# Three seams of a four-stage kernel: a new order in the stencil's last batch, earlier weight and bias loads for attention, and thirty spare matrix products at the very end

## The chip, the cores and the metric

The program runs on one core of one Trainium2 chip. A time is the device time of one execution in microseconds (us); for the kernel before there are three of them and a fourth, profiled execution. Engines are named as the profile names them: PE is TensorE, DVE VectorE, ACT ScalarE, POOL GpSimd and SP SyncE, which here only issues DMAs. DMAs that SP issues all go through one queue (q1 in the profile).

## What is computed

Four layers, one after another, on x of shape (8, 512, 512), all in float32:

```python
# layer 0: a finite-difference step on each 512x512 grid, then max(.., 0)
gradv_Af  = _grad(Af[:, 0], 1) + _grad(Af[:, 1], 2)
gradvv_Bf = _grad2(Bf[:, 0], 1) + _grad2(Bf[:, 1], 2) + _grad(_grad(Bf[:, 2], 2), 1) + _grad(_grad(Bf[:, 2], 1), 2)
x = jnp.maximum(f + (-gradv_Af + gradvv_Bf * 0.5) * dt[:, None, None], 0.0)
# layer 1: attention with an adaptive layer norm (scale and shift from the timestep), bias, mask; then a feed-forward
x = _ln(src) * (1.0 + scale) + shift
q, k, v = x @ Wq + bq, x @ Wk + bk, x @ Wv + bv          # 16 heads of 32
probs = softmax(where(mask, -inf, q k^T / sqrt(32) + attention_bias))
x = x + ((probs v) @ Wo + bo)
x = x + _gelu2((_ln(x) * g2 + beta2) @ W1 + b1) @ W2 + b2
# layer 2: for each batch element one of eight experts: gelu feed-forward, residual, layer norm
# layer 3: hidden + strength * response; response = (hidden @ basis @ basis[:32]^T) @ resp_w^T + biases,
#          basis from two Gram-Schmidt orthogonalisations, strength from a gate on the mean over the rows
```

`_grad` and `_grad2` use one-sided formulas in the first and last row and column, and these make work of their own below.

## The kernel before, in words

The program has three blocks: `stencil` (layer 0), `attention` (the first half of layer 1) and `feed_forwards` (the rest of layer 1 with layers 2 and 3). Between two blocks stands a barrier of all engines. Inside a block each engine runs its own list of instructions, in the order written, and waits on semaphores. No scheduler reorders anything: the Python order of an engine's function is its order on the chip.

**stencil.** The loop goes over the 8 batch elements n. For each, DVE makes the products V, Qp, Qm, Xp, Xm (L508, L593, L595, L512, L513), PE sums them with small band matrices in `acc[n % 2]` (L410 to L425), DVE adds the sum of element n-1 to y (`final(n - 1)`, L532) and makes the centre product y of n (L617, semaphore `s_tf`), and ACT takes the maximum with zero (`relu`, L372, for the last element L368). Rows 0 and 511 of each grid need a one-sided formula. Their ingredients are written to DRAM (`edge(n)`, L244, six small DMAs; `border_pre(n)`, L251, two), collected for four elements at a time (`load_edges`, L270, `load_border_pre`, L276), put together on DVE in 14 tiny steps (`edge_step`, L545 to L553), and stored (`store_borders`, L283). The second of these two groups needs element 7 and so comes at the block's end. `relu(n)` waits until both DMAs of `border_pre(n)` have landed (`s_row`), since it overwrites y; `store(n)` (L257, the last one L261) waits for relu.

The end of this block also prepares attention: SP loads batch 0 of x back in token order into `shared[0]` (L305), the row of scale and shift (L309), Wq into `shared[2]` and Wk into `shared[1]` (L311). DVE takes mean and variance (`first_rows`, L559 to L566), POOL the power -1/2, ACT scales Wq by 1/sqrt(32) (L380) and normalises the rows (L383), and DVE applies scale and shift (L570, L573).

**attention.** Every weight is split into a high part (ACT, `weights_high`, L964) and the rest (DVE, `weights_low`, L1228), and a product is three PE instructions (`split_matmul`, L96 to L98). The opening makes q, k and v of batch 0 and the first scores; then a loop over batch elements and 64 units each runs. Wv and Wo are staged in float32 through `shared[2]` and `shared[1]` after Wq and Wk have left them. DVE scales the q bias by 1/sqrt(32) (L1326) once four POOL-issued DMAs have landed (`s_const`).

**feed_forwards.** 16 passes (8 elements in layer 1, 8 in layer 2) of 16 units; POOL makes high weights (`high`, L1648), DVE the rest (`low`, L1990). DVE normalises the first rows (`ln_apply`, L2017), PE transposes them (L1831). After the last pass come residual, statistics, layer norm (L2055 to L2173), 16 PE transposes (`last_y_transposes`, L1894), high and low parts yH, yL (L1774, L2181), projections to 32 features (L96 to L98), the gate (L1908), and the response rows (L1921, L2200), which SP stores.

Of the kernel before, what the change touches and what calls it, by code (L numbers as in the profile page):

```python
# [38 lines left out]
def f32(ap):  # L39

    return ap.bitcast(F32)
# [73 lines left out]
def stencil(nc, a, x_out, edges, ada_rows, shared, s_rows, s_weights, first):  # L115
# [11 lines left out]
    with ExitStack() as ctx:  # L127
# [57 lines left out]
        s_ndt = sem("dt_negated")  # L185
        s_coef = sem("coefs_made")
# [34 lines left out]
        def _(sp):  # L221
# [62 lines left out]

            for n in range(B):
# [16 lines left out]
            sp.wait_ge(s_sum, B - 1)  # L302
            sp.wait_ge(s_eout[0], 32)
            for r in range(R):
                sp.dma_start(shared[0][:, r, :], tokens_at(x_out, 0)[:, r, :]).then_inc(s_rows[r], 16)  # L305
            sp.wait_ge(s_ada, 16)
            sp.wait_ge(s_tf, B - 1)
            for k, tile in enumerate(first_scale_shift):
                sp.dma_start(tile, ada_rows[0:1, k].to_broadcast([P, D])).then_inc(first.s_ab, 16)  # L309
            for tile, name, loaded in zip(shared[2:0:-1], ("Wq", "Wk"), s_weights):  # L310
                sp.dma_start(tile[:, :, :], a[f"L1_cond_{name}"].rearrange("(k p) n -> p k n", p=P)).then_inc(loaded, 16)  # L311
# [9 lines left out]
        def _(pool):  # L321
# [18 lines left out]
            identity(pool, first.ident, first.s_id)  # L340
            pool.memset(first.mhalf[:, :], -0.5).then_inc(first.s_half, 1)
# [7 lines left out]
        def _(act):  # L349
# [79 lines left out]
        def _(dve):  # L429
# [126 lines left out]
            def first_rows():  # L556
# [9 lines left out]
                dve.tensor_scalar(first.var[:, :], first.mv[:, :, 1], 1e-5, None, ALU.add).then_inc(first.s_var, 1)  # L566
                dve.wait_ge(first.s_ab, 32)
# [14 lines left out]
            for n in range(B):  # L582
# [1733 lines left out]
```

## Time and profile before

| what | value |
|---|---|
| median of 3 executions | 2751.28 us (2749.57 to 2753.77) |
| profiled execution, its own time | 2753.89 us |
| its span in the trace | 2752.2 us |
| PE busy | 2642.5 us, 96% |
| DVE, ACT, POOL busy | 1695.0, 1024.9, 1027.7 us |
| stencil, to attention's first instruction | 0 to 221.4 us |
| attention | 221.4 to about 1187 us |
| feed_forwards, with the tail from 2723.1 | about 1187 to 2752.2 us |

The span counts from the first to the last instruction that the trace shows; the execution's own time is 1.7 us longer. Times below are places in that span. PEclk is the clock that TensorE was granted: 1.00 is 2.4 GHz, 0.50 is 1.2 GHz.

### The profile page before, as it was taken

Reading aid. Unit: us, or ns where it says so; the run is one execution under the profiler, and the core shown is the slowest. Engines: PE = TensorE matmul, PEld = TensorE weight load, DVE = VectorE, ACT = ScalarE, POOL = GpSimd, SP = SyncE. Lnnn points to the kernel's source line nnn. Section 1 sums busy time; section 2 is a strip of 40 time slices with the busy share of each in tenths; the row PEclk is TensorE's granted clock in tenths of the full one; section 3 lists DMA queues with packets and bytes.
Section 4 is the critical chain, followed back from the end, with each engine's and each line's share of the span. In section 5 each row is a group of like instructions: output and inputs, shape, how many; then the busy total and the mean of one; then the engine's idle time right before and its main releaser. Section 6 shows DMA issues by size and latency. Waiting matters only on the chain. (4 is left out here: it accounts for less than half of the span.)

```text
span 2752.2 us, 46368 instructions
## 1 busy us (share of the span) xinstructions
PE 2642.5 (96%) x17096; PEld 2036.1 (74%) x17096; DVE 1695.0 (62%) x3379; ACT 1024.9 (37%) x2161; POOL 1027.7 (37%) x771
## 2 busy tenths in 40 slices
PE   7986999999999999989999999999999999999997
PEld 2434777777777777667888888888787888888775
DVE  8975777777777777765444444445554564565443
ACT  1124666666666666611111111111222323323322
POOL 3003777776777777542101110022222322332210
PEclk9997999999999999999999999999999999999998
DMA  4334564655646456532011001104333243243311
GB/s 169 115 119 149 163 196 139 189 154 174 195 139 190 145 183 183 154 98 77 1 31 31 18 14 31 31 9 124 115 104 119 95 134 124 94 125 127 106 44 39
DMA packets 217922, 306.00 MB, mean 111 GB/s; under 512 B 20450, under 2 KB 98402, under 8 KB 215012
## 3 DMA queue, kind: packets, MB, share of 16 engines
q1 hardware_dynamic: 215954, 302.00, 35.2%
q8 instruction: 138, 2.26, 0.3%
q0 software_dynamic: 1744, 1.04, 0.2%
q14 instruction: 86, 0.70, 0.1%
HBM read 268.94 MB, written 34.04 MB: 110 GB/s over the span
## 5 line engine op out<-in xcount | busy, mean ns | idle before, releaser
L910 POOL TENSOR_TENSOR at_bias<-at_bias,at_mask 128x1024 f32<-128x1024 f32 x220 | 471.7, 2148 | 249.1 <-DMA at_bias<-in_fside_Bx16xSxS 247.7
L1286 DVE CUSTOM_DVE_ANT_0 at_bias<-at_bias,at_bank_score 128x512 f32<-128x512 f32 x512 | 337.8, 680 | 186.2 <-PE at_bank_score L1139 140.8
L96 PE MATMUL ff_bank_out<-ff_WH,ff_gH 128*128 128x512 f32 x1024 | 408.0, 398 | 1.9 <-DVE ff_gL L2037 1.9
L96 PE MATMUL ff_bank_hid<-ff_hH,ff_WH 128*128 128x512 f32 x1024 | 402.7, 393 | 2.7 <-DVE ff_WL L1990 2.6
L1763 ACT ACTIVATE ff_g<-ff_bank_hid,plain_b1c 128x512 f32<-128x512 f32 x256 | 175.6, 686 | 606.2 <-PE ff_bank_hid L98 606.2
L98 PE MATMUL ff_bank_out<-ff_WH,ff_gL 128*128 128x512 f32 x1024 | 400.1, 391 | 0.0
L97 PE MATMUL ff_bank_hid<-ff_hL,ff_WH 128*128 128x512 f32 x1024 | 400.1, 391 | 0.0
L98 PE MATMUL ff_bank_hid<-ff_hH,ff_WL 128*128 128x512 f32 x1024 | 399.6, 390 | 0.0
L97 PE MATMUL ff_bank_out<-ff_WL,ff_gH 128*128 128x512 f32 x1024 | 399.1, 390 | 0.0
L2037 DVE TENSOR_TENSOR ff_gL<-ff_g,ff_gH 128x512 fp32r<-128x512 f32 x256 | 179.0, 699 | 351.1 <-ACT ff_g L1763 346.7
L1648 POOL TENSOR_SCALAR ff_WH<-shared 128x1024 fp32r<-128x1024 f32 x144 | 181.4, 1260 | 564.8 <-PE ff_bank_out L98 346.2
L999 ACT ACTIVATE at_prob<-at_bias,at_nmax 128x512 f32<-128x512 f32 x512 | 366.5, 716 | 20.1 <-DVE at_nmax L1286 19.9
L1146 PE MATMUL at_bank_probT<-first_ident,at_prob 128*128 128x128 f32 x2048 | 313.5, 280 | 5.8 <-ACT at_prob L999 5.4
L1146 PEld LDWEIGHTS at_bank_probT<-first_ident,at_prob 128*128 128x128 f32 x2048 | 228.1, 141 | 94.0 <-issue 67.2
L2035 DVE CAST ff_gH<-ff_g 128x512 fp32r<-128x512 f32 x128 | 70.7, 553 | 359.9 <-ACT ff_g L1763 359.8
L1762 ACT ACTIVATE ff_gH<-ff_bank_hid,plain_b1c 128x512 fp32r<-128x512 f32 x128 | 88.3, 690 | 520.4 <-PE ff_bank_hid L98 520.3
L1007 ACT ACTIVATE at_probT<-at_bank_probT 128x512 f32<-128x512 f32 x256 | 153.2, 598 | 271.1 <-PE at_bank_probT L1146 159.7
L96 PEld LDWEIGHTS ff_bank_hid<-ff_hH,ff_WH 128*128 128x128 f32 x1024 | 193.0, 188 | 45.3 <-DVE ff_WL L1990 3.5
L98 PEld LDWEIGHTS ff_bank_hid<-ff_hH,ff_WL 128*128 128x128 f32 x1024 | 193.0, 188 | 41.1
L98 PEld LDWEIGHTS ff_bank_out<-ff_WH,ff_gL 128*128 128x128 f32 x1024 | 192.5, 188 | 41.6
L97 PEld LDWEIGHTS ff_bank_hid<-ff_hL,ff_WH 128*128 128x128 f32 x1024 | 193.2, 189 | 39.9
L96 PEld LDWEIGHTS ff_bank_out<-ff_WH,ff_gH 128*128 128x128 f32 x1024 | 192.8, 188 | 39.2 <-DVE ff_gL L2037 2.3
(316 smaller groups left out, 4296.0 us busy)
## 6 DMA issues: line engine op xcount, KB each, us to landing
at_bias<-in_fside_Bx16xSxS SPq DMA_DIRECT2D x256, 512.0 KB, 3.8
shared<-in_L_cond_Wi SPq DMA_DIRECT2D x128, 256.0 KB, 2.7
shared<-in_L_cond_Wo SPq DMA_DIRECT2D x128, 256.0 KB, 2.9
shared<-x_after_layer SPq DMA_DIRECT2D x64, 256.0 KB, 5.0
st_f<-in_x SPq DMA_DIRECT2D x8, 1024.0 KB, 7.0
x_after_attention<-shared SPq DMA_DIRECT2D x32, 256.0 KB, 2.6
shared<-in_L_cond_W SPq DMA_DIRECT2D x32, 256.0 KB, 2.9
shared<-x_after_attention SPq DMA_DIRECT2D x32, 256.0 KB, 4.4
```

Source lines behind the costliest of these rows:

```text
L96: pe.matmul(out, wh, xh, start=first, stop=False)
L97: pe.matmul(out, wh, xl, start=False, stop=False)
L98: return pe.matmul(out, wl, xh, start=False, stop=last)
L910: pool.tensor_tensor(bias[i % NB][:, :, :], bias[i % NB][:, :, :], mask[:, i // 2 % R, :].unsqueeze(1).to_broadcast([P, 2, S]), ALU.add).t ...
L999: act.activation(prob[u % 2][:, :], bias[u // 2 % NB][:, u % 2, :], ACT.Exp, scale=-1.0, bias=nmax[:, u % 4:u % 4 + 1], accum_out=sums[:, ...
L1007: act.activation(probT[g % 2][:, j].rearrange("p k q -> p (k q)"), pT[0][:, :], ACT.Copy).then_inc(s_pt[0], 1)
L1146: t = pe.transpose(pT[u % 2][:, k * P:(k + 1) * P], prob[u % 2][:, k * P:(k + 1) * P], ident[:, :])
L1286: dve.tensor_tensor_reduce(t, t, pS[u % HC][:, :], -1.0, 3.0e38, ALU.add, ALU.min, nmax[:, u % 4:u % 4 + 1]).then_inc(s_max, 1)
L1648: pool.tensor_scalar(WH[:, f, :], stage[f % 2][:, :], 1.0, 0.0, ALU.mult, ALU.add).then_inc(s_wh, 1)
L1762: act.activation(gH[f % 2][:, :], pg[f % 2][:, :], func, bias=column).then_inc(s_gh, 1)
L1763: act.activation(g32[f % 2][:, :], pg[f % 2][:, :], func, bias=column).then_inc(s_g32, 1)
L2037: dve.tensor_tensor(gL[f % 2][:, :], g32[f % 2][:, :], f32(gH[f % 2][:, :]), ALU.subtract).then_inc(s_g, 1)
```

## The change

Six edits, at the seams between the blocks.

1. In the stencil SP reloads batch 0 (`load_first_rows`) ahead of `edge(7)`, and loads scale, shift, Wq and Wk (`load_first_weights`) right behind `edge(7)`. Before, both stood behind `store(6)`.
2. DVE takes the first rows' statistics ahead of `final(6)`, applies scale and shift (`scale_first_rows`) behind the centre product of element 7, and runs all 14 edge steps after `final(7)`. Before: statistics, scale and shift, 12 edge steps, `final(7)`, 2 edge steps.
3. ACT normalises the rows ahead of `relu(6)` and scales Wq after it.
4. The q, k and v biases are loaded by POOL at the start of the stencil into a tile that outlives it, and the q bias is scaled in the stencil. Attention's opening waits for them no longer. Wv is loaded as attention's first DMA, into `probT[0]`, which is not yet in use; Wo goes to `shared[2]` as soon as Wq has left it.
5. In feed_forwards POOL starts `high(0)` only after the first rows are normalised, and makes its constants after `high(2)`.
6. Behind the last output product PE runs 30 spare products (`SPARE`) that nobody reads. The tail's high and low parts go to `hH` and `hL`, four buffers each and by then free, so that ACT and DVE wait for no projection.

```diff
+            def load_first_rows():
+                sp.wait_ge(s_sum, B - 1)
+                sp.wait_ge(s_eout[0], 32)
+                for r in range(R):
+                    sp.dma_start(shared[0][:, r, :], tokens_at(x_out, 0)[:, r, :]).then_inc(s_rows[r], 16)
...
             for n in range(B):
                 if n == EG:
                     load_edges(0)
+                if n == B - 1:
+                    load_first_rows()
                 edge(n)
+                if n == B - 1:
+                    load_first_weights()
...
-                if n == B - 1:
-                    act.wait_ge(s_weights[0], 16)
-                    act.activation(shared[2][:, :, :], shared[2][:, :, :], ACT.Copy, scale=1.0 / math.sqrt(HD)).then_inc(first.s_ws, 1)
+                if n == B - 2:
                     act.wait_ge(first.s_rstd, 2)
...
+                if n == B - 1:
+                    act.wait_ge(s_weights[0], 16)
+                    act.activation(shared[2][:, :, :], shared[2][:, :, :], ACT.Copy, scale=1.0 / math.sqrt(HD)).then_inc(first.s_ws, 1)
                 relu(n)
...
+                if n == B - 1:
+                    first_rows()
                 if n > 0:
                     final(n - 1)
...
-            first_rows()
-            for k in range(12):
-                edge_step(1, k)
+            scale_first_rows()
             final(B - 1)
-            for k in range(12, 14):
+            for k in range(14):
                 edge_step(1, k)
...
+            load_weight(2, "Wv")
             load_mask(0)
             for i in range(3):
                 load_bias(0, i)
-            for k, name in ((2, "Wv"), (3, "Wo")):
-                sp.wait_ge(s_wl, k - 1)
-                sp.dma_start(stage[k], a[f"L1_cond_{name}"].rearrange("(k p) n -> p k n", p=P)).then_inc(s_w[k], 16)
+            sp.wait_ge(s_wl, 1)
+            load_weight(3, "Wo")
...
-            act.wait_ge(s_const, 64)
             weights_high(2)
-            act.wait_ge(s_bq, 1)
...
             first_highs = highs_by(-1)
+            pool.wait_ge(s_xn, 1)
             high(0)
             high(1)
...
+                pe.wait_ge(s_fin, n * R)
+                for k in range(SPARE):
+                    pe.matmul(pt[1][:, :], WH[:, k % FC, 0:P], WH[:, k % FC, D:2 * D], start=True, stop=True)
                 pe.wait_ge(s_h, BATCHES * C)
...
-                    if not (isinstance(n, int) and n == 0 and m < 2):
+                    if not alone(n) and not (n == 0 and m < 2):
                         act.wait_ge(s_chunk, n * C + max(m - 1, 0))
```

SP's queue in the stencil's last batch, before (border_rows is the DRAM scratch of the border rows, st_eo and st_ep the collected ones; the six rows of `edge(7)` come first):

```order
L244 DMA border_rows<-st_Qm 4x8x64
L244 DMA border_rows<-st_Qp 4x8x64
L244 DMA border_rows<-st_V 4x8x64
L251 DMA border_rows<-st_y 8x1x64 x2
L257 DMA x_after_layer<-st_y 128x2048
L305 DMA shared<-x_after_layer 128x512 x4
L309 DMA st_B<-scale_shift_rows 128x512 x2
L311 DMA shared<-in_L_cond_Wq 128x4x512
L311 DMA shared<-in_L_cond_Wk 128x4x512
L270 DMA st_eo<-border_rows 32x768 x2
```

The same place now:

```order
L290 DMA shared<-x_after_layer 128x512 x4
L245 DMA border_rows<-st_Qm 4x8x64
L245 DMA border_rows<-st_Qp 4x8x64
L245 DMA border_rows<-st_V 4x8x64
...
L296 DMA st_B<-scale_shift_rows 128x512 x2
L298 DMA shared<-in_L_cond_Wq 128x4x512
L298 DMA shared<-in_L_cond_Wk 128x4x512
L252 DMA border_rows<-st_y 8x1x64 x2
L258 DMA x_after_layer<-st_y 128x2048
L271 DMA st_eo<-border_rows 32x768 x2
```

The reload and the weights have moved ahead of `border_pre(6)` (st_y to border_rows) and of the store of element 6.

DVE at the end of the stencil, before, from `final(6)` on:

```order
L532 SCALAR_TENSOR_TENSOR st_y<-st_bank_sum,st_dtb,st_y 128x2048
L617 TENSOR_TENSOR st_y<-st_B,st_f 128x2048
L559 BN_STATS first_stats<-shared 128x6 x4
...
L570 TENSOR_TENSOR shared<-shared,st_B 128x512 x4
L573 TENSOR_TENSOR shared<-shared,st_B 128x512 x4
L545 TENSOR_SCALAR st_eacc<-st_eo,st_ew 64x64
L547 SCALAR_TENSOR_TENSOR st_eacc<-st_eo,st_ew,st_eacc 64x64 x11
L532 SCALAR_TENSOR_TENSOR st_y<-st_bank_sum,st_dtb,st_y 128x512 x2
```

And now:

```order
L571 BN_STATS first_stats<-shared 128x6 x4
...
L580 TENSOR_SCALAR first_bc<-first_bc 128x4
L544 SCALAR_TENSOR_TENSOR st_y<-st_bank_sum,st_dtb,st_y 128x2048
L635 TENSOR_TENSOR st_y<-st_B,st_f 128x2048
L586 TENSOR_TENSOR shared<-shared,st_B 128x512 x4
L589 TENSOR_TENSOR shared<-shared,st_B 128x512 x4
L544 SCALAR_TENSOR_TENSOR st_y<-st_bank_sum,st_dtb,st_y 128x512 x2
L544 SCALAR_TENSOR_TENSOR st_y<-st_bank_sum,st_dtb,st_y 128x1024
L557 TENSOR_SCALAR st_eacc<-st_eo,st_ew 64x64
```

The statistics stand ahead of `final(6)`, and the edge steps behind `final(7)`.

## Rows read from the trace of the kernel before

**Rows 1.** Windows: us, busy PE, PEld, DVE, ACT, POOL, then PEclk, DMA, GB/s.

```profile
191.00:194.50 3.50, 2.58 (x7) 0.79 (x5) 3.33 (x10) 0.00 (x0) 0.00 (x0) 1.00 1.00 341
```

**Rows 2.** Timeline of SP's queue, stencil's end: start, us, what.

```profile
180.95 1.27 SPq L251 DMA_DIRECT2D border_rows<-st_y  x2
...
185.73 2.99 SPq L305 DMA_DIRECT2D shared<-x_after_layer  x4
...
216.36 1.44 SPq L283 DMA_DIRECT2D x_after_layer<-st_ep  x2
221.36 0.41 SPq L816 DMA_DIRECT2D at_m<-in_mask_Bx1xSxS_bk  x1
```

**Rows 3.** Timeline of PE, DVE and ACT, stencil's end.

```profile
169.39 3.60 PE L425 MATMUL st_bank_sum<-st_Xm,st_mats 128*128 128x512 f32 x8
...
183.37 1.91 ACT L372 ACTIVATE st_y<-st_y 128x2048 f32<-128x2048 f32 x1 [15.59 <-DMA border_rows<-st_y]
...
189.99 3.60 PE L425 MATMUL st_bank_sum<-st_Xm,st_mats 128*128 128x512 f32 x8
...
191.03 2.72 DVE L559 BATCH_NORM_STATS2 first_stats<-shared 128x6 f32<-128x512 f32 x4 [7.91 <-DMA shared<-x_after_layer]
...
198.04 1.91 ACT L380 ACTIVATE shared<-shared 128x2048 f32<-128x2048 f32 x1 [12.77 <-DMA shared<-in_L_cond_Wq]
...
206.23 3.49 DVE L547 SCALAR_TENSOR_TENSOR st_eacc<-st_eo,st_ew,st_eacc 64x64 f32<-64x64 f32 x11
209.88 2.60 DVE L532 SCALAR_TENSOR_TENSOR st_y<-st_bank_sum,st_dtb,st_y 128x512 f32<-128x512 f32 x3 [0.16 <-issue]
...
215.82 0.28 DVE L551 SCALAR_TENSOR_TENSOR st_ep<-st_eacc,st_edt,st_ep 64x64 f32<-64x64 f32 x1 [3.35 <-issue]
```

**Rows 4.** DMA issues: KB each, us from issue to landing.

```profile
shared<-in_L_cond_Wk SPq DMA_DIRECT2D x1, 1024.0 KB, 11.7
...
st_eo<-border_rows SPq DMA_DIRECT2D x2, 96.0 KB, 10.6
```

**Rows 5.** DMA issues over the whole run, the same columns.

```profile
shared<-in_L_cond_Wo SPq DMA_DIRECT2D x1, 1024.0 KB, 5.3
```

**Rows 6.** Timeline of attention's opening.

```profile
230.83 0.17 DVE L1326 TENSOR_SCALAR at_bc<-at_bc 128x4 f32<-128x4 f32 x1 [2.69 <-DMA at_bob<-in_L_cond_bo]
...
233.34 0.47 PE L96 MATMUL at_bank_proj<-at_xH,at_WH 128*128 128x512 f32 x1 [2.13 <-DVE at_WL L1228]
...
233.81 1.91 ACT L964 ACTIVATE at_WH<-shared 128x2048 fp32r<-128x2048 f32 x1 [6.19 <-DMA shared<-in_L_cond_Wv]
...
241.80 0.75 DVE L1298 TENSOR_SCALAR at_vT<-at_bank_proj,at_bc 128x512 f32<-128x512 f32 x1 [2.37 <-PE at_bank_proj L98]
```

**Rows 7.** Windows of half a microsecond in attention's opening.

```profile
233.50:234.00 0.50, 0.50 (x2) 0.40 (x2) 0.00 (x0) 0.19 (x1) 0.00 (x0) 0.67 0.00 0
```

**Rows 8.** Line L2017 and its instructions, all passes: durations in ns.

```profile
L2017 DVE TENSOR_SCALAR ff_xn<-shared,first_mv,first_rstd x32: 528/541/1418, 1189.5 to 1819.8; 128x512 f32<-128x512 f32 x32
```

**Rows 9.** Timeline of feed_forwards' opening.

```profile
1189.55 4.23 DVE L2017 TENSOR_SCALAR ff_xn<-shared,first_mv,first_rstd 128x512 f32<-128x512 f32 x4 [1.97 <-PEq L68]
...
1193.70 2.27 DVE L1990 TENSOR_TENSOR ff_WL<-shared,ff_WH 128x1024 fp32r<-128x1024 f32 x1
```

**Rows 10.** Windows around the last output product and in the tail.

```profile
2650.00:2660.00 10.00, 10.00 (x48) 8.00 (x47) 2.58 (x4) 3.46 (x8) 0.00 (x0) 1.00 0.00 0
...
2725.00:2725.50 0.50, 0.00 (x0) 0.00 (x0) 0.50 (x2) 0.00 (x0) 0.00 (x0) 0.90 0.00 0
```

**Rows 11.** Timeline of the tail.

```profile
2730.58 0.45 PE L1894 MATMUL ff_bank_tr<-first_ident,shared 128*128 128x128 f32 x1 [7.30 <-DVE shared L2173]
...
2733.62 0.60 ACT L1774 ACTIVATE ff_yH<-ff_bank_tr 128x512 fp32r<-128x512 f32 x1 [12.96 <-PE ff_bank_tr L1894]
...
2736.68 0.60 ACT L1774 ACTIVATE ff_yH<-ff_bank_hid 128x512 fp32r<-128x512 f32 x1 [1.78 <-PE ff_bank_tr L98]
...
2740.15 0.95 PE L1908 MATMUL ff_bank_tr<-ff_pooled,ff_w1g 128*128 128x1 f32 x8
```

More of the change, by code:

```diff
@@ L283, in store_borders, with load_first_weights @@
                     sp.dma_start(x_out[g * EG:(g + 1) * EG, e * (S - 1), :].rearrange("b (q c) -> q b c", q=QS), ep[part, :]).then_inc(s_eout[g], 16)
+            def load_first_rows():
[3 more added lines that the diff above has]
+                    sp.dma_start(shared[0][:, r, :], tokens_at(x_out, 0)[:, r, :]).then_inc(s_rows[r], 16)
+            def load_first_weights():
+                sp.wait_ge(s_ada, 16)
+                sp.wait_ge(s_tf, B - 1)
+                for k, tile in enumerate(first_scale_shift):
+                    sp.dma_start(tile, ada_rows[0:1, k].to_broadcast([P, D])).then_inc(first.s_ab, 16)
+                for tile, name, loaded in zip(shared[2:0:-1], ("Wq", "Wk"), s_weights):
+                    sp.dma_start(tile[:, :, :], a[f"L1_cond_{name}"].rearrange("(k p) n -> p k n", p=P)).then_inc(loaded, 16)
             for n in range(B):
@@ L301, in _ @@
                     sp.dma_start(f[n % 2][:, :, :], rows_of(a["x"][n + 2])).then_inc(s_f[n % 2], 16)
[L302 to L311, printed above, removed]
             load_edges(1)
@@ L340, in _ @@
             identity(pool, first.ident, first.s_id)
+            for k, name in enumerate(("bq", "bk", "bv")):
+                pool.dma_start(first.bc[:, k, :], a[f"L1_cond_{name}"].rearrange("(c p) -> p c", p=P), allow_slow_non_contiguous=True).then_inc(s_bc, 16)
             pool.memset(first.mhalf[:, :], -0.5).then_inc(first.s_half, 1)
@@ L566, in first_rows, with scale_first_rows @@
                 dve.tensor_scalar(first.var[:, :], first.mv[:, :, 1], 1e-5, None, ALU.add).then_inc(first.s_var, 1)
+                dve.wait_ge(s_bc, 48)
+                dve.tensor_scalar(first.bc[:, 0, :], first.bc[:, 0, :], 1.0 / math.sqrt(HD), None, ALU.mult)
+            def scale_first_rows():
                 dve.wait_ge(first.s_ab, 32)
@@ L679, in attention @@
         probT = [sb(f"probT{s}", [P, HC, R, P]) for s in range(2)]
-        bc = sb("bc", [P, 3, C])
+        bc = first.bc
         bob = sb("bob", [P, D])
@@ L1406, in feed_forwards @@
         stats, mv, var, rstd = plain.norm
-        mhalf = sb("mhalf", [P, R])
+        mhalf = first.mhalf
         g2c = plain.g2c
@@ L1534, in y_bank, with y_parts @@
             return (pt[0], pg[0], pg[1], po[0])[m] if alone(n) else pt[0]
+        def y_parts(n, m):
+            return (hH[:, m, :], hL[:, m, :]) if alone(n) else (yH[m % 2][:, :], yL[m % 2][:, :])
         @blk.sync
@@ L1711, in _ @@
                                a[name].rearrange("(c p) r -> p c r", p=P)).then_inc(s_uv, 16)
-            for g in range(2, first_highs):
+            high(2)
+            pool.memset(ones[:, :], 1.0).then_inc(s_cm, 1)
+            pool.memset(phalf[:, :], 0.5).then_inc(s_cm, 1)
+            pool.memset(later[:, :, :], 1.0).then_inc(s_cm, 1)
+            pool.wait_ge(s_cm, 3)
+            pool.affine_select(out=later[:, :, :], in_=later[:, :, :], compare_op=ALU.is_ge, fill=0.0, base=-1,
+                               pattern=[[-1, RANK], [1, RANK]], channel_multiplier=0).then_inc(s_cm, 1)
+            for g in range(3, first_highs):
                 high(g)
@@ L1773, in tail @@
                         act.wait_ge(s_g1, n)
[L1774 removed]
+                    act.activation(y_parts(n, m)[0], y_bank(n, m)[:, :], ACT.Identity,
                                    accum_out=pooled[:, m:m + 1]).then_inc(s_yh, 1)
@@ L2178, in tail @@
                     dve.wait_ge(s_yh, n * C + m + 1)
-                    if not (isinstance(n, int) and n == 0 and m < 2):
+                    if not alone(n) and not (n == 0 and m < 2):
                         dve.wait_ge(s_chunk, n * C + max(m - 1, 0))
-                    dve.tensor_tensor(yL[m % 2][:, :], y_bank(n, m)[:, :], f32(yH[m % 2][:, :]), ALU.subtract).then_inc(s_yl, 1)
+                    high_, low_ = y_parts(n, m)
+                    dve.tensor_tensor(low_, y_bank(n, m)[:, :], f32(high_), ALU.subtract).then_inc(s_yl, 1)
                 if f == 9:
```

27 lines of the change are left out of this document (9 added, 18 removed).

## The prediction

> **What bounds the kernel now.** I first read the page. PE is busy 96% of the span, so the long middles of attention and of the feed-forwards are PE's, and the diff adds or removes nothing there. What it touches are four places where PE stands still: the end of the stencil, attention's opening, the feed-forwards' opening, and the tail. So I read each of these by the timeline, with the waits in brackets, then half-microsecond windows for the clock and the DMA list for landings.
>
> *Stencil's end.* PE finishes element 7's sums at 193.6 [rows 3]. `final(7)`, which needs only them, starts at 209.88, so DVE is 16.3 late. Why: the reload of batch 0 is issued only at 185.73 [rows 2], behind the store of element 6; the statistics wait for it until 191.03; ACT waits for Wq until 198.04 before it may normalise; scale, shift and 12 edge steps follow (the 11 long ones take 3.49) [rows 3]. From `final(7)` to attention's first DMA at 221.36 are 11.5.
>
> *Attention's opening.* DVE waits 2.69 for constants, PE 2.13 for the low part of Wk, ACT 6.19 for Wv. The v projection is evacuated at 241.80 [rows 6].
>
> *Feed-forwards' opening.* `ln_apply` takes 4.23 for four rows [rows 9], where the median over all passes is 0.541 a row [rows 8]. It runs beside POOL's `high(0)`.
>
> *Tail.* The clock is 1.00 after the last product at 2723.1 and falls at 2725.4 (0.90 in a window of 0.5) [rows 10]. So the 16 transposes and most of the 12 projections run at 1.2 GHz. ACT waits 1.78 for a buffer in between [rows 11].
>
> **The change, part by part.**
>
> *A. Stencil's end.* In the new order SP's reload needs the sums of element 6, which PE has at about 173.0 (its last eight products start at 169.39 and take 3.60 [rows 3]). That is 12.7 ahead of 185.73. Four DMAs take 2.99 to issue [rows 2]; the six of `edge(7)` follow, then scale, shift, Wq, Wk, until about 181.8. The statistics run in DVE when it used to begin `final(6)`: ten instructions, 3.33 [rows 1], with the q bias 3.5. `final(6)` ended before at 180.95, where its two border DMAs start [rows 2]; now at 184.4, and the centre product at 186.7. ACT, behind POOL's power, normalises from about 183.5 to 186.5 (it ran from the end of Wq's scaling at 199.95 [rows 3] and took about 3), and DVE scales and shifts until 191.9, both before 193.6. So `final(7)` follows PE directly: 193.7 to 196.3, its 2.60 [rows 3]. That would shift the block's end by 16.2.
>
> But something else is late next. `border_pre(6)` is now issued at 184.5, behind 2.5 MB of scale, shift, Wq and Wk. Wk landed 11.7 after its issue with other loads ahead, and the 96 KB of st_eo behind it took 10.6 [rows 4], though small DMAs alone land sooner: relu(6) followed the first border DMA at 180.95 by 2.4, at 183.37 [rows 2, 3]. Small DMAs thus wait out what is ahead of them. At 341 GB/s [rows 1] 2.6 million bytes take 7.7; from 180.3 with about 2 of latency they land at 190, so relu(6) starts at about 191, not 183.37. Behind it on ACT stand the scaling of Wq and relu(7); behind `store(6)` on SP stand st_eo's load, `border_pre(7)` and store(7). relu(6) ends at 193.1, store(6) is issued, st_eo's load lands behind that 1 MB (the 1 MB of Wo took 5.3 alone [rows 5]) at about 198.5, twelve edge steps and two more end at about 202.8. Before, border stores were issued at 216.36 [rows 2]. **A is -13.5.** Bounds: if the small DMAs pass the large ones, relu(6) is off the path, the edge steps follow `final(7)` at 196.3 and end at 200.6: -15.8. If Wq and Wk take 3 longer with the edges' writes, everything behind shifts: -10.5.
>
> The Trainium skill, DMA: Bandwidth & Descriptors, section on queues, rings and completion order, says that each DMA engine consumes a ring's descriptors in order, which speaks against putting two megabytes ahead of a small store that gates relu. By that rule the sum is the -13.5; st_eo's 10.6 agrees with it [rows 4].
>
> *B. Attention's opening.* DVE's low part of Wk began at 230.9, after the bias; now it follows the rows' low parts, whose end lies 2.69 ahead of 230.83: 228.1, done at 230.4. PE is done with q at about 231.2 and goes on without its 2.13. Wv, issued first, lands after some 5.3 [rows 5] at 226.7, so ACT splits it from 227.6 rather than from 233.81, and DVE follows to 232.7. The v projection then needs only the q evacuation (about 233.5), starts at 234 to 235 and ends at about 237. Against 241.80 [rows 6] that is 5 at best. The clock decides the rest: it fell to 0.67 in the window from 233.5 [rows 7], behind the gap of 2.13. If it is low for all of k, 12 products cost 2.4 more. I take **-4.5**, between -3 and -5.5. Masks and the first bias tiles now land behind 1 MB of Wv, by 236 at the latest; they are first needed at about 240, which hides them. Without that cover up to 3 would return.
>
> *C. Feed-forwards' opening.* Alone, the four rows take 4 x 0.541 = 2.2 instead of 4.23 [rows 8, 9]: 2.1 gained for PE's transposes. `low(0)` took 2.27 beside POOL's constants [rows 9]; now it runs beside `high(1)`. Of the 2.1 part goes back: the mask of the Gram-Schmidt step (`later`) now comes after `high(2)`, which waits for a DMA. I estimate it ready about 1 after PE asks for it. **-1.0**, between +0.5 and -2.
>
> The Trainium skill, SBUF — State Buffer, section on the two separate sides, says that DVE's two-input instructions and GpSimd's reads take a shared port exclusively, so that `low(0)` would wait for all of `high(1)`. By that alone C would be about 0; the trace's 4.23 against 2.2 is of that sort, but for another instruction [rows 8, 9].
>
> *D. Tail.* 30 products at the 48 in 10 us of steady state [rows 10] take 6.3 to 6.8, so from 2723.1 to 2729.9, and the transposes need their first row at 2730.58 [rows 11]: the spares hide wholly in DVE's statistics and layer norm. If they ran at half clock they would take 13 and cost 6. With the clock up, the last row's transposes lie behind DVE's last row, not behind PE's backlog: yH starts 0.8 earlier than 2733.62. Then ACT and DVE run through four chunks with no wait, 0.6 each, and PE needs three products of 0.21 to 0.23 per chunk instead of 0.43 each. The gate starts at about 2737.0, not 2740.15 [rows 11]: -3.1. With the clock low again all through, only the buffers help, and the gate's own products slow down: -0.3. PE idles some 0.6 before the transposes and 1.2 before the projections. A gap of 2.13 in attention's opening preceded a fall [rows 6, 7]. The tail's gaps are shorter, but there are several. I take **-2.2**.
>
> Sum: -13.5 - 4.5 - 1.0 - 2.2 = -21.2. The profiled execution was 2753.89, which makes 2732.7; it lies 2.6 above the median of the runs, so on the median 2751.28 the forecast is 2730.1, rounded to 2730.
>
> **The rivals.**
> 1. *The small stores don't queue, so relu(6) is early.* For it: nothing shows this very pair. Against it: st_eo's 10.6. A is -15.8, the time 2728. Chance 15%.
> 2. *The tail's clock falls anyway*, since idle gaps come between transposes and projections. For it: the fall at 2725.4 and the one at 233.7 [rows 7, 10]. D is -0.5, the time 2732. Chance 30%.
> 3. *Queueing costs more than I count*: relu(6) 4 to 6 later, since reads of 2 MB and the reload meet, and the same again for the last border loads. A is about -8, the time 2736. Against it: the queue moved 341 GB/s there [rows 1]. Chance 10%.
> 4. *Slower.* relu(6) gates the block's end. Its chain from relu(6)'s start to the end is 17 by my sum, so 221.36 is reached if it starts at 204.7. To make the kernel slower by 0.2% it must also eat B to D and 5.5, a start near 218, 33 after its store's issue. The longest landing here is 11.7 [rows 4]. Chance 2%.
> 5. *Openings don't pay*: another wait takes the place of the removed ones in B, for instance k's bank or Wv's landing (11.7 for Wk [rows 4]), and C loses to its mask. Sum about -15, the time 2736. Chance 8%.
>
> My own forecast has 35%.
>
> **How the numbers follow.** The range takes the bounds: all best, -15.8 - 5.5 - 2 - 3.1 = -26.4, is 2725; all worst short of rival 4, -8 - 3 + 0.5 - 0.3 = -10.8, is 2740.5. Both ends need four things at once, so I keep 2724.5 below, for runs that scatter by 2, and 2738 above. A change under 0.2% (5.5 us) can't be told from none here. Every case but rival 4 is past that; I leave 3% for a gain under 5.5.
>
> **What would show it.** In the new trace: `final(7)` starts within 0.5 of PE's last sum; relu(6) waits for its border DMA until about 191 (rival 1: 187); attention's first DMA is at about 207.9; the v evacuation comes 15.9 after it, where it was 20.4; `ln_apply` takes 2.2; the clock is 1.00 through the spare products, and the gate starts about 14 after the last output product, where it was 17. I am wrong if store(6) lands so late that ACT's relu(7) or SP's last loads set a longer chain, or if the middle of attention runs at another pace.

## The result

| | us |
|---|---|
| before, median of 4 runs taken beside it | 2752.53 (2749.57 to 2754.82) |
| after, median of 4 runs | 2730.64 (2727.61 to 2735.28) |
| ratio, 95% interval | 0.9923 (0.9903 to 0.9942) |

The change took 21.9 us; the forecast, 2730.0 in a range of 2724.5 to 2738.0, holds. The profiled execution of after took 2733.09, with a span of 2731.4, so between the two traces 20.8 lie. They show where.

**The stencil's end.** Timelines of after, first SyncE's queue, then ScalarE and VectorE, then the landings (KB each, us from issue to landing); they answer to [rows 2 to 4].

```profile
172.44 1.75 SPq L290 DMA_DIRECT2D shared<-x_after_layer  x4
...
179.48 0.51 SPq L298 DMA_DIRECT2D shared<-in_L_cond_Wk  x1
183.53 1.31 SPq L252 DMA_DIRECT2D border_rows<-st_y  x2
...
190.39 1.30 SPq L271 DMA_DIRECT2D st_eo<-border_rows  x2
...
205.68 0.41 SPq L840 DMA_DIRECT2D at_probT<-in_L_cond_Wv  x1
```

```profile
188.00 1.91 ACT L383 ACTIVATE st_y<-st_y 128x2048 f32<-128x2048 f32 x1 [2.38 <-DMA border_rows<-st_y]
...
193.12 2.60 DVE L544 SCALAR_TENSOR_TENSOR st_y<-st_bank_sum,st_dtb,st_y 128x512 f32<-128x512 f32 x3 [2.60 <-PE st_bank_sum L437]
...
200.10 0.28 DVE L563 SCALAR_TENSOR_TENSOR st_ep<-st_eacc,st_edt,st_ep 64x64 f32<-64x64 f32 x1 [0.58 <-DMA st_ep<-border_rows]
```

```profile
shared<-in_L_cond_Wk SPq DMA_DIRECT2D x1, 1024.0 KB, 8.9
...
st_eo<-border_rows SPq DMA_DIRECT2D x2, 96.0 KB, 4.4
```

`final(7)` now waits for PE and for nothing else. `border_pre(6)` is the row at 183.53, whose stores gate relu(6). relu(6), in ACT's first row, starts 4.5 behind the issue of its border store, where it took 2.4 before [rows 2, 3]; Wk landed at 188.4 (179.48 + 8.9), within half a microsecond of it. Attention's first DMA is at 205.68, 15.7 earlier than 221.36 [rows 2]. These places move from profile to profile: in the nine that have this order on SyncE's queue it lies between 205.1 and 207.3, in the four that have the old one between 220.8 and 221.7.

**Attention's opening.** The windows show the granted clock (PEclk, third from last); before, it was low again from 233.7 to 237 and once more from 247 to 251.

```profile
221.40 0.75 DVE L1312 TENSOR_SCALAR at_vT<-at_bank_proj,first_bc 128x512 f32<-128x512 f32 x1 [2.15 <-PE at_bank_proj L98]
```

```profile
206.00:208.00 2.00, 2.00 (x10) 2.00 (x11) 0.31 (x1) 2.00 (x2) 0.91 (x2) 0.50 0.38 60
209.00:236.00 27.00, 20.97 (x119) 14.59 (x122) 18.39 (x30) 14.24 (x27) 8.39 (x4) 1.00 0.60 206
```

The v evacuation comes 15.7 behind the first DMA, before 20.4 [rows 6].

**The feed-forwards' opening**, timeline; it answers to [rows 9].

```profile
1167.05 1.91 DVE L2037 TENSOR_SCALAR ff_xn<-shared,first_mv,first_rstd 128x512 f32<-128x512 f32 x4 [2.09 <-PEq L68]
1169.11 3.99 PE L1848 MATMUL ff_bank_tr<-first_ident,ff_xn 128*128 128x128 f32 x16 [5.01 <-DVE ff_xn L2037]
...
1170.26 2.05 DVE L2010 TENSOR_TENSOR ff_WL<-shared,ff_WH 128x1024 fp32r<-128x1024 f32 x1 [1.30 <-POOL ff_WH L1664]
...
1173.73 0.77 PE L96 MATMUL ff_bank_hid<-ff_hH,ff_WH 128*128 128x512 f32 x1 [0.64 <-DVE ff_hL L2049]
...
1179.98 1.33 POOL L1727 TENSOR_SCALAR_AFFINE_SELECT ff_later<-ff_later 128x1024 f32<-128x1024 f32 x1
...
1180.22 1.63 DVE L2057 TENSOR_TENSOR ff_gL<-ff_g,ff_gH 128x512 fp32r<-128x512 f32 x1
...
1181.77 0.41 DVE L2095 TENSOR_TENSOR ff_prod<-uv 128x256 f32<-128x256 f32 x1
...
1182.28 1.08 PE L1887 MATMUL ff_bank_tr<-ff_prod,ff_ones 128*128 128x64 f32 x8 [0.86 <-issue]
...
1183.16 0.48 PE L96 MATMUL ff_bank_out<-ff_WH,ff_gH 128*128 128x512 f32 x1
```

The rows take 1.91 instead of 4.23 and PE's transposes follow 2.06 after their start instead of 4.38. But VectorE then waits 1.30 for POOL, and PE 0.86 ahead of the first gram product (the small product `ff_prod` times ones that opens a Gram-Schmidt step). POOL had finished the mask at 1181.31 (1179.98 + 1.33), before PE came to this wait at 1181.42; what PE waited for is VectorE's `ff_prod`, which ended at 1182.18, 0.10 ahead of PE's start. It was late because VectorE's split ahead of it took 1.63 beside POOL's select, where it takes 0.69 alone. The first output product comes 16.11 behind the rows' start; before it was 15.77 (1205.32 less 1189.55).

**A seam in the middle**, where the diff adds nothing: PE's wait for VectorE's product in the last dense pass, and two windows, of the gap and behind it.

```profile
1860.92 1.97 PE L1887 MATMUL ff_bank_tr<-ff_prod,ff_ones 128*128 128x64 f32 x8 [2.54 <-DVE ff_prod L2095]
```

```profile
1857.00:1860.50 3.50, 1.38 (x7) 0.80 (x5) 2.34 (x6) 0.69 (x1) 1.92 (x1) 1.00 0.11 38
1861.00:1867.00 6.00, 6.00 (x18) 5.10 (x19) 2.17 (x4) 0.00 (x0) 0.00 (x0) 0.50 0.44 146
```

The trace of before has the same wait at 1881.9, 1.6 long, and the clock stays at 1.00 behind it.

**The tail**, timeline and two windows; they answer to [rows 10, 11].

```profile
2705.39 6.96 PE L1907 MATMUL ff_bank_tr<-ff_WH 128*128 128x512 f32 x30
...
2712.86 0.30 PE L1914 MATMUL ff_bank_tr<-first_ident,shared 128*128 128x128 f32 x1 [0.51 <-DVE shared L2193]
...
2719.38 0.95 PE L1928 MATMUL ff_bank_tr<-ff_pooled,ff_w1g 128*128 128x1 f32 x8
```

```profile
2705.50:2712.30 6.80, 6.80 (x31) 5.33 (x29) 6.53 (x16) 0.00 (x0) 1.45 (x1) 1.00 0.00 0
2712.80:2715.20 2.40, 2.33 (x16) 1.68 (x16) 1.90 (x3) 0.08 (x1) 0.00 (x0) 1.00 0.00 0
2716.60:2719.40 2.80, 2.80 (x13) 1.41 (x14) 1.73 (x3) 0.94 (x4) 0.00 (x0) 1.00 0.03 6
```

The spare products end before the first transposed row is ready, the clock is 1.00 throughout, and the gate starts 14.0 behind the last output product's end, before 17.05.

Placed on one line, the lead of after over before is 15.7 at attention's first DMA, 20.4 at the v evacuation, 22.9 at attention's last product, 22.2 at the first output product, 17.7 at the last one and 20.8 at the gate and at the end. So 4.4 were lost again between the first and the last output product. The experiments take this apart.

### The profile page after: what moved, and what is told of

It is laid out like the page before. It is cut to its first block and busy times, and to the rows that moved or that the text cites. A ratio compares the mean times of both kernels' runs of the same rounds, so it can differ in the third digit from the quotient of the medians.

```text
span 2731.4 us, 46406 instructions
## 1 busy us (share of the span) xinstructions
PE 2643.7 (97%) x17109; PEld 2039.0 (75%) x17126; DVE 1696.5 (62%) x3379; ACT 1025.1 (38%) x2161; POOL 1025.8 (38%) x770
## 3 DMA queue, kind: packets, MB, share of 16 engines
q0 software_dynamic: 1744, 1.04, 0.2%
```

## The experiments

Each kernel is read by a distance inside its trace, in the stage that it changes, and not by the total alone, which other stages disturb by several microseconds. Of e5 to e8 there is one time each (2730.23, 2734.14, 2730.96, 2730.32, with one of before at 2749.11), of e10 and e11 as well (2726.20 and 2733.68); they say little, the traces more.

**The four parts, each alone on the kernel before.** The edits are those of the change's list: 1 to 3 without the bias lines (e1), 4 (e2), 5 (e3), 6 (e4). In e1 for example:

```diff
+                if n == B - 1:
+                    load_first_rows()
                 edge(n)
+                if n == B - 1:
+                    load_first_weights()
...
-            first_rows()
-            for k in range(12):
-                edge_step(1, k)
+            scale_first_rows()
             final(B - 1)
```

e1, the stencil's end alone. 

> The kernel before with the change of the stencil's end alone (A), without the bias loads. The prediction's theory for A, small stores wait out the 2 MB ahead of them, gave -13.5 and attention's first DMA at 207.9. The changed kernel's trace had it at 205.7, which is -15.7, rival 1's number. If that is A's own doing, the first DMA is again at 205 to 206.5 here, relu(6) starts at 187 to 189, and the time is 15 to 16.5 below before. If the other parts helped it (the bias loads, for instance), the first DMA is at 207 or later and the gain is 12.5 to 14.

e2, attention's opening alone. 

> The kernel before with the change of attention's opening alone (B). Theory: the v projection is evacuated 15.7 after attention's first DMA, where before it was 20.4, so at least -4.7; and since PE no longer idles in the opening for 2.1 us at a stretch, TensorE's clock does not fall to half in it twice, which the changed kernel showed as a further -2.4 by attention's end: -7 in the time. Rival: the clock's falls come and go with the run, so only the chain's -4.7, or less, stands in the time; the granted clock of the stretch from 12 to 30 after the first DMA tells (1.00 throughout, or 0.50 in places).

e3, the feed-forwards' opening alone. 

> The kernel before with the change of POOL's order in the feed-forwards' opening alone (C). The prediction gave -1.0. By the changed kernel's trace the four rows of layer norm take 1.9 rather than 4.2 and PE's transposes start 2.2 earlier, but the first hidden product comes 4.6 after them rather than 3.6 (VectorE's low part of the weights waits for POOL's high part, which now starts only behind the layer norm), and PE waits 0.9 for POOL's mask before the first gram product. Theory: the first output product comes 11.0 to 11.8 after VectorE's layer norm ends plus nothing saved, so the total is between -1.0 and +1.0, which is no change that can be told. Rival: the loss seen came from the clock's phase, and alone the part is worth its -2.

e4, the tail alone. 

> The kernel before with the change of the tail alone (D). Theory: the 30 spare products keep the clock at 1.00 until the gate, the gate's products start 14.0 after the last output product's end instead of 17.0, and the time is 3.0 lower. The prediction had taken -2.2, and its rival 2 (the clock falls anyway) -0.5: then the granted clock is 0.50 in the stretch of the transposes or projections, and the gate starts 16 to 16.7 after the last output product.

| | median us | before beside it | ratio (95%) | its own stage |
|---|---|---|---|---|
| e1 | 2737.61 | 2753.72 | 0.9942 (0.9928 to 0.9955) | first DMA at 205.11: -16.25 |
| e2 | 2748.98 | 2753.72 | 0.9991 (0.9982 to 1.0) | v evacuation 15.27 behind it: -5.2 |
| e3 | 2753.44 | 2753.72 | 1.0004 (0.9995 to 1.0013) | first output product 16.12 behind the rows' start: +0.35 |
| e4 | 2750.48 | 2753.72 | 0.9986 (0.9976 to 0.9995) | gate 14.2 behind the last output product's start, before 17.25: -3.05 |

Timelines of e1 and of e2, a window of e2's opening, and e3's timeline:

```profile
188.69 1.91 ACT L380 ACTIVATE st_y<-st_y 128x2048 f32<-128x2048 f32 x1 [2.51 <-DMA border_rows<-st_y]
...
205.11 0.41 SPq L827 DMA_DIRECT2D at_m<-in_mask_Bx1xSxS_bk  x1
```

```profile
221.15 0.41 SPq L829 DMA_DIRECT2D at_probT<-in_L_cond_Wv  x1
...
236.42 0.75 DVE L1301 TENSOR_SCALAR at_vT<-at_bank_proj,first_bc 128x512 f32<-128x512 f32 x1 [1.25 <-PE at_bank_proj L98]
```

```profile
230.60:236.40 5.80, 5.78 (x26) 4.46 (x24) 3.06 (x3) 1.38 (x2) 3.57 (x2) 1.00 0.95 355
```

```profile
1204.60 1.08 PE L1871 MATMUL ff_bank_tr<-ff_prod,ff_ones 128*128 128x64 f32 x8 [1.04 <-POOL ff_later L1711]
```

e1 gives A all of its gain by itself, with relu(6) at 188.7, as its theory had it. In e2 PE has no gap where it had 2.13, and the clock is 1.00 up to the evacuation and on to 30 behind the first DMA; the four kernels with the old opening (before, e1, e3, e4) all show it at 0.50 for some 3 us or more there, from 11 or 12 behind the first DMA. In e3 the profile names the late mask as the releaser of the gram product, but there too the select had ended at 1203.63, 0.97 before it, and `ff_prod` ended at 1204.50, 0.10 before it. The medians agree with their own stages within 0.1 to 0.6. e3 shows no gain, as its theory had it, and e4 the 3.0 of its theory.

e2's stage gained what both of its sides allowed, but its median is 4.7 below before and not the 7 of its theory, and the interval reaches 1.0. Its eleven runs lie in two groups, six from 2746.70 to 2748.98 and five from 2752.68 to 2753.35: something 4 to 5 us wide comes and goes. The profiles of all kernels show what can: in the ten with the new opening the evacuation lies 14.9 to 15.75 behind the first DMA (in the four with the old one 20.4 to 21.9) and the clock is 1.00 up to it, but in seven of the ten (not in after, e2 and e10) it falls to 0.50 for 3 to 4 us from about 21 behind the first DMA.

The old tail isn't the same in every profile either. The clock had fallen 2.3 to 2.5 behind the last output product in before, e2 and e3, and the gate came 17.25 behind that product's start; in e1, with the same tail, it fell 4.7 behind it, was back at 1.00 before the projections, and the gate came at 16.05. Against e1 the new tail is worth 1.85 and not 3.05.

**e5: who stands ahead in SyncE's queue.** The changed kernel, with one call moved.

```diff
                 edge(n)
-                if n == B - 1:
-                    load_first_weights()
...
                     border_pre(n - 1)
+                    if n == B - 1:
+                        load_first_weights()
                     store(n - 1)
```

> The changed kernel with SyncE's scale, shift, Wq and Wk loads issued behind the border stores of element 6 instead of ahead of them. Theory (queueing is real, but hidden): the border store of element 6 no longer stands behind 2 MB, so relu(6) starts 2.4 to 2.7 after its issue instead of 4.5, at 185.5 to 186.5 (in the changed kernel 188.0), Wq lands at 190 to 192 and its scaling runs then, and still the stencil's block ends where it did, attention's first DMA at 205.2 to 206.2, since the chain PE's last sums, final(7), edge steps, border stores holds the end. The prediction's theory (relu(6) gates the end through store(6) and the edge rows' load): the first DMA comes earlier by what relu(6) gains, 1.5 to 2.5, at 203.2 to 204.2.

The first DMA came at 207.87: neither theory's number, and 2.2 later than in the changed kernel (35.1 behind the reload's issue, where the nine profiles of the changed order have 32.1 to 33.4). Timeline of ScalarE and VectorE, and the landings:

```profile
186.28 1.91 ACT L383 ACTIVATE st_y<-st_y 128x2048 f32<-128x2048 f32 x1 [0.34 <-DMA border_rows<-st_y]
```

```profile
190.27 2.50 DVE L586 TENSOR_TENSOR shared<-shared,st_B 128x512 f32<-128x512 f32 x4 [4.24 <-DMA st_B<-scale_shift_rows]
192.68 2.49 DVE L589 TENSOR_TENSOR shared<-shared,st_B 128x512 f32<-128x512 f32 x4
195.09 2.59 DVE L544 SCALAR_TENSOR_TENSOR st_y<-st_bank_sum,st_dtb,st_y 128x512 f32<-128x512 f32 x3
199.49 0.25 DVE L557 TENSOR_SCALAR st_eacc<-st_eo,st_ew 64x64 f32<-64x64 f32 x1 [1.81 <-issue]
```

```profile
st_eo<-border_rows SPq DMA_DIRECT2D x2, 96.0 KB, 10.0
```

relu(6) did start early, 2.43 behind its store's issue. So the queueing was real. But the scale now lands so late that VectorE's scaling pushes `final(7)` 1.7 behind PE, and the 96 KB of st_eo, which landed in 4.4 when Wk was already in, take 10.0 behind it and hold the edge steps. Whoever stands behind the two megabytes waits; in the changed kernel that is relu(6), which has the time.

**e6 and e7: the tail's two halves.** The changed kernel without the spare products (`SPARE = 0`), and with them but on the old buffers:

```diff
-            return (hH[:, m, :], hL[:, m, :]) if alone(n) else (yH[m % 2][:, :], yL[m % 2][:, :])
+            return (yH[m % 2][:, :], yL[m % 2][:, :])
```

> The changed kernel without the 30 spare products, but with the tail's separate buffers hH, hL. Theory (the clock is what pays): without them the clock falls some 2.5 after the last output product, the transposes and projections run at half clock, and the gate's products start 16.0 to 16.7 after the last output product's end (before 17.0, changed kernel 14.0). Rival (the buffers pay, the clock hardly): the gate starts 14.0 to 14.8 after it though the granted clock is 0.50.

> The changed kernel with the 30 spare products, but with the two alternating buffers yH, yL and their waits, as before. Theory: the clock is 1.00 through the projections, ScalarE's third copy waits 0.7 to 1.0 for the first chunk's projection to be read (in the kernel before 1.78 at half clock), and the gate starts 14.7 to 15.5 after the last output product's end: of the tail's 3.05 some 2 are the clock's and 1 the buffers'. Rival (only the clock pays): no wait before the third copy and the gate at 14.0 to 14.2.

One row and one window of e6, then one row of e7:

```profile
2720.12 0.95 PE L1928 MATMUL ff_bank_tr<-ff_pooled,ff_w1g 128*128 128x1 f32 x8
```

```profile
2710.00:2719.00 9.00, 7.01 (x24) 4.64 (x25) 5.36 (x9) 2.42 (x8) 0.00 (x0) 0.50 0.00 0
```

```profile
2714.31 0.60 ACT L1791 ACTIVATE ff_yH<-ff_bank_hid 128x512 fp32r<-128x512 f32 x1 [1.18 <-PE ff_bank_tr L98]
```

The ruler is from POOL's rstd, 3.9 behind the last output product, to the gate: before 2727.03 to 2740.15, that is 13.12; e6 12.54; e7 11.13; changed kernel 10.08. The gate thus starts some 16.5 and 15.05 behind the last output product's end, in both as the first theory had it. Two details came otherwise: in e6 the clock fell 5.4 behind the last output product and not 2.5, and in e7 ScalarE's third copy waited 1.18 and not 0.7 to 1.0. The clock is worth 2.0 with the old buffers and 2.5 with the new, the buffers 0.6 at half clock and 1.05 at full.

**e8 and e10: POOL's order in the feed-forwards' opening.** e8 moves the constants (`ones`, `phalf`, `later`) from behind `high(2)` to ahead of it. e10:

```diff
-            pool.wait_ge(s_xn, 1)
             high(0)
+            pool.wait_ge(s_xn, 1)
             high(1)
```

> The changed kernel with POOL's constants (ones, phalf, the mask later) made right behind the DMA issues and ahead of high(2), which waits for a weight load anyway. Theory (the late mask is part of what ate C's gain): PE no longer waits 0.9 to 1.0 for the first gram product, VectorE's first split of the hidden activations is not slowed (0.43 and 0.69 instead of 0.72 and 1.63), and the first output product starts 18.5 to 19.0 after the attention's last product did (changed kernel 19.7, kernel before 19.0). Rival (contention only moves): POOL's memset and select now run beside VectorE's splits of the layer norm's output, which then take 1.2 to 1.6 instead of 0.69, the first hidden products start later, and the first output product comes no earlier than 19.4.

> The changed kernel with POOL's wait for the layer norm's output moved behind high(0), so that the high part of the first weights is made beside VectorE's four rows again. Theory: the rows take 2.3 to 3.0 instead of 1.91, but VectorE's low part starts right behind them, without the 1.30 that it waits now, so the first hidden product starts at most 0.6 us later or up to 0.9 earlier than in the changed kernel, counted from the start of the rows (6.7 there); my estimate is 0.5 earlier. Rival (the two engines take turns, so that every microsecond beside POOL is lost to VectorE): the rows take 2.9 or more and the first product starts no earlier than 6.7 after them.

Timeline of e8, then of e10:

```profile
1174.79 1.34 POOL L1726 TENSOR_SCALAR_AFFINE_SELECT ff_later<-ff_later 128x1024 f32<-128x1024 f32 x1
1175.04 1.63 DVE L2049 TENSOR_TENSOR ff_hL<-ff_h,ff_hH 128x512 fp32r<-128x512 f32 x1
...
1176.72 0.80 PE L96 MATMUL ff_bank_hid<-ff_hH,ff_WH 128*128 128x512 f32 x1 [1.64 <-DVE ff_hL L2049]
...
1185.39 0.48 PE L96 MATMUL ff_bank_out<-ff_WH,ff_gH 128*128 128x512 f32 x1
```

```profile
1165.82 2.78 DVE L2037 TENSOR_SCALAR ff_xn<-shared,first_mv,first_rstd 128x512 f32<-128x512 f32 x4 [2.09 <-PEq L68]
...
1181.42 0.47 PE L96 MATMUL ff_bank_out<-ff_WH,ff_gH 128*128 128x512 f32 x1
```

e8 goes to its rival. PE's wait ahead of the first gram product is gone, and VectorE's first split of the hidden activations takes 0.69 again, but the select falls on VectorE's splits (1.63 for a split of 0.69), PE has gaps of 1.17 and 1.64 among its first products, the clock, just risen, falls again at 1176, and the first output product comes 21.5 behind attention's last product, 1.8 later than in the changed kernel. e10: the rows take 2.78, the first hidden product comes 6.57 behind their start (6.68 in the changed kernel) and the output product 15.60 (16.11). The direction of the theory, at a fifth of my estimate for the hidden product. PE's wait ahead of the gram product is 0.45 here; the mask was ready 2.4 before it, and `ff_prod` had waited 0.84 for the load of V.

**e9: the seam.** The changed kernel, and in `gram_schmidt` on PE:

```diff
+                    if n == B - 1 and f == 5:
+                        pe.wait_ge(s_gcopy, i)
+                        for k in range(8):
+                            pe.matmul(pt[1][:, :], WH[:, 4 + k % 2, 0:P], WH[:, 4 + k % 2, D:2 * D], start=True, stop=True)
                     pe.wait_ge(s_prod, i + 1)
```

> The changed kernel with eight spare products on PE ahead of its wait for VectorE's product in the last low-rank step but two (unit 5 of the last dense batch). In the profiles so far PE waits there 1.1 to 2.5 us, and in two of six (the changed kernel, and the tail alone) the clock fell to 0.50 behind that wait for about 7 us; those two took 852 to 853 from the first feed-forward's rstd to the first gate, the others 846.5 to 849. Theory (this seam's fall is what separates the changed kernel's runs at 2727 to 2728 from those at 2733 to 2735): with the gap filled the clock is 1.00 there in every run, the median is 2727 to 2729.5 and no run is above 2731.5. Rival (falls depend on more than this gap): the runs scatter as before, with a part of them at 2732 to 2735, and the median is 2730 to 2731.5.

Timeline of e9:

```profile
1860.53 1.10 PE L1891 MATMUL ff_bank_tr<-ff_prod,ff_ones 128*128 128x64 f32 x8 [0.44 <-DVE ff_prod L2099]
```

The median is 2728.11 of five, against 2752.93 before (0.9914, 0.9900 to 0.9927), and the seam is at 1.00. From the first feed-forward's rstd to the first gate are 846.7; over all profiles it is 846.5 to 849.9 in twelve, and 853.1 and 852.2 in the two where the clock fell there for 6 to 7 us (the changed kernel and e4). So the seam is where the changed kernel's profile lost its 4.4. The four kernels that share this code with it and did not fall there (e5, e7, e8, e10) took 846.6 to 848.3. But filling the seam does not hold the clock elsewhere: e12 has the same spares and 1.00 at the seam, fell to 0.50 some 65 us later and took 849.9. And the highest of the five runs is 2732.02, above the 2731.5 that the theory allowed, and the interval does not tell this kernel from the changed one. That the clock was 1.00 at the seam in every run isn't shown; only the profiled run shows its clock there.

**e11 and e12: more spares, and all together.** e11 adds eight 128x128 products of the identity while PE waits for the first rows. e12 has four of these, the seam's, e10's order, and PE's gram product waiting for `ones` alone (the mask is waited for on VectorE).

> The changed kernel with eight spare 128x128 products of the identity on PE at the start of the feed-forwards' block, while it waits for VectorE's first rows. Theory: PE begins some 2 us earlier, so its clock rises about 2 us earlier than 1177.1 (which was 10.1 after the rows' start at 1167.05), at 8 to 8.5 after it, and the first output product comes 0.7 to 1.2 earlier than 16.1 after the rows' start. Rival (the rise comes by its own pace, whatever a few small products add): the rise stays at 9.5 to 10.5 after the rows' start and the output product at 15.9 to 16.3.

> The changed kernel with four repairs together: the eight spare products at the seam; POOL's high(0) ahead of its wait; PE's first gram product waiting only for ones, and VectorE for the mask where it uses it; four small spare products of the identity while PE waits for the first rows. Theory: the opening's terms add, so the first output product comes 14.3 to 15.0 after the rows' start (changed kernel 16.1, first high free alone 15.6: the mask's wait of 0.45 to 0.9 and some 0.5 of half clock go), the seam shows the clock at 1.00, and the median is 2725.5 to 2728 against the changed kernel's 2730.6. Rival (what limits the opening is VectorE, so no wait moved off PE shortens it): the first output product stays at 15.4 to 16.0, and the median is that of the seam spares alone, 2727.5 to 2728.5.

A window of e11 and a row of e12's timeline:

```profile
1172.00:1184.00 12.00, 9.24 (x43) 5.80 (x40) 10.71 (x16) 5.67 (x7) 7.64 (x10) 1.00 0.73 216
```

```profile
1183.57 0.42 DVE L2102 TENSOR_TENSOR ff_prod<-uv 128x256 f32<-128x256 f32 x1 [1.34 <-DMA uv<-in_L_cond_V]
```

In e11 the clock rose 3.5 behind the rows' start instead of 10.9 (it was at 1178.0 in the changed kernel, not at 1177.1), far earlier than the theory had it, and the output product still came at 16.36. Here PE did wait 1.51 for the mask: VectorE's low part had started first, and POOL's select took 2.18 instead of 1.33. The same happened in e5 and e9, whose openings are the changed kernel's, with the output product at 16.35 and 16.36; where POOL came first and VectorE's split took 1.6 (after, e3, e6, e7) it was at 16.1. The eight products also took 3.6 and held the transposes back 1.4.

e12 missed both of its ranges: the output product is at 16.18, and the median 2728.73 (0.9910, 0.9897 to 0.9924). Taking the mask off PE could bring nothing beyond e10, since e10's wait was for V already; in e12 VectorE waits 1.34 for that load, then PE 0.96. Neither kernel is shown to beat the changed one.

## Why the prediction was right, point by point

*A, -13.5 forecast, -15.7 in the trace of after and -16.25 alone.* The queueing was as forecast, but the chain that I put last was not last. The step was "from 180.3 with about 2 of latency they land at 190, so relu(6) starts at about 191", and behind it store(6), st_eo and twelve edge steps to 202.8. In fact SyncE reached scale and shift at 178.1, not 180.3, one reason being that the reload's four DMAs took 1.75 to issue and not 2.99; Wk landed 10.3 behind that, at 188.4, where I had counted 9.7; and relu(6) started with that landing, at 188.0, not 1 behind it. With these 3 us won, st_eo landed at 194.8, ahead of the first edge step at 195.75, and the chain through relu(6) was no longer the last. What holds the end is the one that I had as rival 1's: PE's sums, `final(7)`, edge steps, with 0.58 of waiting for st_ep. So the number that rival 1 gave for A came true and its reason, that small stores pass large ones, did not: e5 refutes it, with 2.43 against 4.5 for the same store and 10.0 against 4.4 for st_eo. The Trainium skill, DMA: Bandwidth & Descriptors, section on queues, rings and completion order, says that an engine takes a ring's descriptors in order; the runs agree. Rival 3, more queueing, did not come.

*B, -4.5 forecast, -4.7 and -5.2.* Right in size and in the main in its reason: the evacuation is 15.7 and 15.3 behind the first DMA, 15.9 was said. In after PE still waits 1.07 for the low part of Wk, where I had it go on without a wait. I had left open whether the clock falls in the opening; up to the evacuation it did not in any of the ten profiles without the gap of 2.13, but in seven of them it fell some 6 us later.

*C, -1.0 forecast, +0.35 at the first output product, in after and alone.* The step that failed is "Of the 2.1 part goes back". All of it went. The transposes start 2.3 earlier and the first hidden product 1.3 earlier, since `low(0)` waits 1.30 for a `high(0)` that now starts behind the rows. That low part then took 2.05 beside POOL's `high(1)`, where it takes 1.21 alone (e10). The clock rises 10.1 behind the rows' start before and 10.9 after (1199.6 and 1178.0), so the products that came earlier ran at half of it. Then PE waits 0.86 to 1.04. I had put a wait of 1 there, for the mask; the size was right and the cause was not, in these two traces: the mask was ready before PE asked, and PE waited for `ff_prod`, behind a split that took 1.63 instead of 0.69 beside the mask's making. The Trainium skill, SBUF — State Buffer, section on the two separate sides, has the two engines exclude each other at a shared port; by it I had worked out about 0, and the splits of 1.63 for 0.69 beside POOL's select, in after and in e8, agree with it, as does the select of 2.18 for 1.33 behind VectorE's start in e11. The rule was nearer than my own number.

*D, -2.2 forecast, -3.05 in after and alone.* The mechanism was right and I discounted it for a fall that did not come: the clock stays at 1.00 across PE's idle stretches of 0.5 and 1.2, and rival 2, which I had given 30%, is out in both profiles. My undiscounted working, 3.1, is what was measured against before, e2 and e3; against e1, whose old tail ran 1.2 shorter, it is 1.85. e6 and e7 give the split: 2.0 to 2.5 are the clock's and 0.6 to 1.05 the buffers'.

*The sum.* The stages add to -15.7 - 4.7 + 0.35 - 3.05 = -23.1, more than the -21.2 forecast; the medians show 21.9 and the two traces 20.8. Between lie two things outside the four stages: the changed kernel's trace gained some 2.4 between the evacuation and attention's last product, where that of before had the clock down from 247 to 251, and lost 4.4 in the middle of the feed-forwards. The first differs between profiles of one opening (e5 to e9 fall there, after does not), and so does the second. Whether the tail's edit makes the seam's wait longer is open: it is 2.06 to 3.39 in the profiles that have that edit and no spares there, and 1.12, 1.50, 1.59 and 2.49 in those without. That the time came within 0.6 of the forecast is in part such luck: A and D were too small by 3 together, C too large by 1.4.

Rival 5, openings that don't pay, was right for C and wrong for B. Rival 4, slower, never came near: relu(6) would have had to wait to 218 and started at 188.

What stays open: whether a gap makes the clock fall. At the seam it fell behind waits of 2.54, 2.06 and 3.39 (the last in e11), and behind 2.42 in e6, for 4 us; not behind 2.49 (e2), 2.12 (e10), and 2.25 to 2.40 (e5, e7, e8). Nothing tried tells these apart.

## What to carry to other kernels

When a large load is moved ahead of small ones on the same queue, everything small behind it waits out its bytes, so put ahead of it what the last chain needs and behind it what has slack; in e5 the other order freed relu(6) by 2.1 and brought attention's first DMA 2.2 later. An engine that was made to wait its turn so that another may run alone must be followed to its own next product: here the gain of 2.3 was gone 14 us later, in a low part, a slow clock and splits slowed by POOL. When a profile names a releaser, look at when that instruction ended: here the mask that it named in e3 was done 0.97 earlier. Spare products that lie wholly in an idle stretch before a chain of small matrix products were worth 2.0 to 2.5 us here, and less where the clock came back by itself (e1); judge such an edit by a distance inside the trace, since totals scatter more than it brings.

## What the runs showed of the hardware that was not expected

- The clock's falls come and go between profiles, at places where the code is the same, and with them 846.5 to 853.1 for the same stretch of feed-forwards in fourteen profiles. The four runs of after go with it: 2727.61 and 2728.18 at a mean granted clock of 0.993 and 0.992, 2733.09 and 2735.28 at 0.991. That e2's two groups come from it isn't shown.
- How soon it rises varies widely: 10.1 to 10.9 behind the rows' start with PE idle ahead of them (before, e3, after), 3.5 with small identity products in front (e11).
- A VectorE instruction that only reads one tile is slowed by POOL too: the four rows take 1.91 alone, 2.78 beside one POOL pass (e10) and 4.23 beside two and the constants [rows 9].
- The same 96 KB load took 4.4, 10.0 and 10.6, by what stood ahead of it.
